# Edge stage of a graph attention kernel: a gather that waits for Q, and one weighed head moved from VectorE to GpSimd in every second pair

## The chip, the core and the metric

One core of a Trainium2 chip runs the whole program. Its engines work side by side, each through its own list of instructions, and wait for one another only by semaphores: TensorE (PE; loading of weights is shown as PEld), VectorE (DVE), ScalarE (ACT), GpSimd (POOL) and SyncE (SP), which issues DMAs. GpSimd and ScalarE issue DMAs too. The metric is the time of one execution on the device in microseconds (us), the median of several runs. Beside it stands one execution taken by the hardware profiler, whose trace is read here.

## What is computed

```python
N, D = x.shape                                   # 6250, 512
Q = (x @ Wq).reshape(N, H, d)                    # H = 8 heads of d = 64
K = (x @ Wk).reshape(N, H, d)
V = (x @ Wv).reshape(N, H, d)
src, dst = (edge_index[0], edge_index[1])        # 106250 edges, sorted by dst
score = jnp.einsum('ehd,ehd->eh', K[src], Q[dst]) * scale
score = jnp.exp(jnp.clip(score, -5.0, 5.0))[..., None]
msg = V[src] * score
wV = jax.ops.segment_sum(msg, dst, num_segments=N)
Z = jax.ops.segment_sum(score, dst, num_segments=N)
h_attn = (wV / (Z + 1e-06)).reshape(N, D)
h = x + h_attn                                   # then batch norm over the nodes, plus x,
                                                 # then layer norm of each row
```

All inputs are float32. Half of the edges go each way, and every node has a loop to itself.

## The kernel before

Three stages follow one another. `project` computes Q, K and V of all 49 tiles of 128 nodes and stores K and V side by side in `kv_d`, 4 KB a node. `attend` is the edge stage. `normalise` divides by Z and computes both norms. The change is in `attend`.

The edges lie in blocks of 128, one edge to a partition. A block that touches two tiles of destinations is visited twice, so there are 879 visits, taken in 440 pairs. A pair q uses slot q % 8 of a ring of eight in SBUF: `kv` holds for each of its two blocks the gathered K (512 numbers), V (512) and 8 weights. A name such as `s_g`, `s_seg`, `s_v` or `s_exp` is a family of eight semaphores, one for each slot; `s_qx` is a single one that counts pairs. The loop bodies are unrolled over the eight slots. For pair q the engines do this:

- GpSimd, `step` (line 752): two gathers, `gather(q, s, fills, 0)` and the same with u = 1, each an indirect DMA of 128 rows of 4 KB (line 747). Before the first it waits until the slot is free, which is when PE has accumulated pair q-8 (`s_seg`). Every fourth pair it copies indices. After the second gather it weighs, for even pairs only, one head of the pair that is five back (POOL_LAG): V times weight, `weigh`, line 710.
- PE, `step` (line 898): in step q it spreads the rows of Q over the edges of pair q+1 (two blocks, four matmuls into `q_ps`, line 915), once pair q has been multiplied, since `q_ps` has one buffer; this is counted in `s_qx`. Every second step it expands the bits of destinations (`mm_ps`, lines 925 and 927). Then it accumulates pair q-2 (`acc`, line 940), once all its heads are weighed: it waits for `s_v` to reach 3 a filling for even pairs (ScalarE, VectorE, GpSimd), 2 for odd ones. A record of the trace is half of such a float32 matmul, so one pair has eight.
- VectorE, `step` (line 783): it multiplies K by Q for pair q (line 791, waits for `s_g` and `s_qx`), clips the scores of q-1 (line 795), weighs heads of q-2 (line 710: three heads for even pairs, four for odd ones) and sums K times Q for pair q by head (line 802).
- ScalarE: exp of the scores (line 856), and four heads of both blocks weighed (line 842, eight instructions a pair); every second pair the matrices of zeros and ones (line 852), and for each tile that is complete the copy out of `acc`.

SyncE loads the tiles of Q, two of which are held. All of this order is written out by hand; nothing reorders it.

Of the kernel before, what the change touches and what calls it, by code (L numbers as in the profile page):

```python
# [32 lines left out]
N_NODES, DIM, HEADS = 6250, 512, 8  # L33
# [47 lines left out]
def wait_apart(eng, sem, value):  # L81


    if not isinstance(value, int):
        value = eng.snap(eng.to_reg(value))
        eng.wait_ge(sem, 1)
    wait(eng, sem, value)
# [538 lines left out]
def attend(nc, block, kv_d, q_d, lb_d, nb_d, xb_d, tabs, agg, rz, kv, first, x_first, s_first, s_slots, soft):  # L626
    lb, nb, q_tile, zeros, less, eps = first
    src_t, bits_row, cnt_row, ident = tabs
    with ExitStack() as ctx:
# [28 lines left out]
        s_nb, s_q = soft["s_nb"], soft["s_q"]  # L658
        s_qx, s_evc, s_evict = (soft[n] for n in ("s_qx", "s_evc", "s_evict"))
        s_rz = soft["s_rz_early"]  # L660
        POOL_LAG = 5
        LOOKAHEAD, LAG = 4, 3

        def pipeline(eng, step, head):
# [70 lines left out]
        def _(pool):  # L735
# [6 lines left out]
            def gather(q, s, fills, u):  # L742
                if u == 0:
                    if s % IDX_PAIRS == 0:
                        wait_apart(pool, s_idx[s // IDX_PAIRS], fills)
                    wait_apart(pool, s_seg[s], fills - 1)
                pool.indirect_dma_start(kv[:, s, u, 0:2 * DIM], None, kv_d,  # L747
                                        bass.IndirectOffsetOnAxis(idx[:, s, u:u + 1], 0),
                                        bounds_check=N_NODES - 1, oob_is_err=False
                                        ).then_inc(s_g[s], 16)  # L750

            def step(q, s, fills):
                p = q - POOL_LAG
                sp, fp = at(s, fills, -POOL_LAG)
                if there(q):
                    gather(q, s, fills, 0)
                if there(q + 2) and s % IDX_PAIRS == IDX_PAIRS - 2:
                    index(q + 2, *at(s, fills, 2))
                if there(q):
                    gather(q, s, fills, 1)  # L760
                if s % 2 and there(p):
                    wait_apart(pool, s_exp[sp], fp)
                    weigh(pool, sp, HEADS - POOL_HEADS, POOL_HEADS).then_inc(s_v[sp], 1)
            pool.wait_ge(soft["s_trc"], 1)
# [13 lines left out]
        def _(dve):  # L778
# [4 lines left out]
            def step(q, s, fills):  # L783
# [12 lines left out]
                                      ALU.min).then_inc(s_clip[s1], 1)  # L796
                if there(q - 2):
                    dve.wait_ge(s_exp[s2], f2)
                    weigh(dve, s2, ACT_HEADS, HEADS - ACT_HEADS - (POOL_HEADS if s % 2 == 0 else 0)).then_inc(s_v[s2], 1)
                if there(q):  # L800
                    dve.wait_ge(s_mul[s], fills)
                    dve.tensor_reduce(raw[:, s, :, :], heads(kv[:, s, :, 0:DIM]), AX.X,  # L802
# [78 lines left out]
        def _(pe):  # L881
# [16 lines left out]
            def step(q, s, fills):  # L898
# [32 lines left out]
                if there(c):  # L931
                    tiles = [pe.snap(tile_regs[(2 * sc + u) % PLACES], min_val=0, max_val=TILES - 1)
                             for u in range(2)]
                    pe.wait_ge(s_v[sc], (2 if sc % 2 else 3) * fc)
                    pe.wait_ge(s_evict, tiles[1] + 1)
                    for u in range(2):
                        par = tiles[u] % 2
# [442 lines left out]
```

## Time and profile before

| | us |
|---|---|
| median of 3 runs | 2098.77 |
| lowest, highest | 2097.2, 2105.61 |
| the profiled execution, time on the device | 2113.25 |
| the profiled execution, its span | 2111.5 |
| first to last start of VectorE's line 791 (edge stage) | 463.9 to 1959.1 |

| engine | busy us | share of the span |
|---|---|---|
| PE | 1918.3 | 91% |
| VectorE | 1696.9 | 80% |
| ScalarE | 1377.7 | 65% |
| GpSimd | 1249.1 | 59% |

The span is from the first to the last instruction of the profiled execution, 1.75 us less than its time on the device. The page sums up this execution in parts: busy time by engine, the chain of work that ended last, and groups of instructions by source line. The views of the trace give single instructions in order of time, the waits, and the busy time in any stretch. In a row, "[0.79 <-PE q_ps L915]" says that the engine had been idle for 0.79 us and that an instruction of line 915 on PE ended the wait, as far as the trace tells. The ends of matmuls are modelled. Where the profile names no releaser it writes "issue" or "remote".

### The profile page before, as it was taken

The page shows a single profiled execution, that of the slowest core. Times are in us where ns is not written, and L with a number is a line of the kernel's source. Part 1 is how long each engine was busy: PE and PEld are TensorE (multiplying, and loading weights), DVE is VectorE, ACT ScalarE, POOL GpSimd, SP SyncE. Part 2 cuts the span into 40 slices and gives each one's busy share as a digit, 9 for nine tenths or more (in the row PEclk, how much of TensorE's full clock was granted, in tenths as well). Part 3 has the DMA queues.
Part 4 walks back from the last instruction along what each step waited for, and adds up shares of the span by engine and source line. Part 5 has one row for each costly group of instructions (what it writes and reads, how often), then busy time and mean ns, then how long its engine had stood idle before and what let it go on. Part 6 is the DMA issues. An engine that isn't in the chain of part 4 may idle for free.

```text
span 2111.5 us, 41623 instructions
## 1 busy us (share of the span) xinstructions
PE 1918.3 (91%) x7904; PEld 1351.1 (64%) x8014; DVE 1696.9 (80%) x2454; ACT 1377.7 (65%) x4602; POOL 1249.1 (59%) x1473
## 2 busy tenths in 40 slices
PE   7999999989998998998899899898899899899887
PEld 4555555547776776776677677676676677677433
DVE  6676655538888888888888888888888888888988
ACT  0001000018887887887888888788788788788866
POOL 0106663026666666666666666666666666666657
PEclk9999999999999999999999999999999999999999
DMA  4648886358998898888888989898899899889607
GB/s 172 176 147 299 293 301 237 143 206 300 315 326 291 304 322 307 313 305 309 306 307 305 325 315 311 301 314 300 296 321 309 294 317 320 307 300 331 225 0 289
DMA packets 184521, 589.09 MB, mean 279 GB/s; under 512 B 28480, under 2 KB 30240, under 8 KB 184480
## 3 DMA queue, kind: packets, MB, share of 16 engines
q0 software_dynamic: 135904, 465.14, 63.5%
q1 hardware_dynamic: 45120, 121.69, 16.2%
q10 hardware_dynamic: 3456, 1.78, 0.3%
q8 instruction: 18, 0.29, 0.1%
q14 instruction: 23, 0.19, 0.0%
HBM read 535.27 MB, written 78.91 MB: 291 GB/s over the span
## 4 chain that ended last, share of the span: by engine, by line
PE 70%; DVE 16%; issue 7%; another core or an unknown queue 2%; ACT 2%; DMA 1%; POOL 1%; SPq 0%; DVEq 0%; ACTq 0%; POOLq 0%
PE q_ps L915 26%; PE places L342 20%; PE acc L940 19%; DVE kv L791 11%; PE mm_ps L925 2%; DVE stats L1278 1%; DVE agg L1262 1%; ACT agg L1189 1%; DVE raw L802 1%; PE mm_ps L927 1%; DVE agg L1271 1%; PE places L402 1%; PE banks L1132 1%; DMA kv<-kv_d,idx 1%
## 5 line engine op out<-in xcount | busy, mean ns | idle before, releaser
L747 POOL DMA_INDIRECT kv<-kv_d,idx x880 | 891.9, 1014 | 548.9 <-issue 214.0
L842 ACT ACTIVATE kv<-kv 128x64 f32<-128x64 f32 x3520 | 888.9, 335 | 14.3
L940 PE MATMUL acc<-kv,mm_sb 128*128 128x260 f32 x3520 | 852.1, 385 | 11.9 <-issue 4.4
L940 PEld LDWEIGHTS acc<-kv,mm_sb 128*128 128x128 f32 x3520 | 672.8, 192 | 114.3 <-issue 10.7
L791 DVE TENSOR_TENSOR kv<-q_ps,kv 128x1024 f32<-128x1024 f32 x440 | 536.4, 1219 | 214.7 <-PE q_ps L915 161.1
L915 PE MATMUL q_ps<-q_tile,mm_sb 128*128 x1760 | 550.0, 434 | 146.0 <-DVE kv L791 114.7
L802 DVE TENSOR_REDUCE raw<-kv 128x16 f32<-128x1024 f32 x440 | 532.7, 1211 | 0.0
L915 PEld LDWEIGHTS q_ps<-q_tile,mm_sb 128*128 128x128 f32 x1760 | 316.9, 190 | 285.3 <-DVE kv L791 193.6
L852 ACT ACTIVATE mm_sb<-mm_ps,less 128x1024 fp32r<-128x1024 f32 x220 | 241.5, 1098 | 66.2 <-remote 60.1
L710 DVE TENSOR_TENSOR kv<-kv 128x384 f32<-128x384 f32 (+1 forms) x440 | 271.8, 618 | 0.0
L856 ACT ACTIVATE kv<-raw 128x16 f32<-128x16 f32 x440 | 92.0, 209 | 197.9 <-DVE raw L795 181.8
L342 PE MATMUL places<-t_sb,s_sb 128*128 128x512 f32 (+1 forms) x552 | 185.5, 486 | 0.0
L435 ACT COPY p<-places 128x768 f32<-128x768 f32 x23 | 18.4, 799 | 247.8 <-PE places L342 247.8
L342 PEld LDWEIGHTS places<-t_sb,s_sb 128*128 128x128 f32 x552 | 104.8, 190 | 73.6 <-issue 66.5
L710 POOL TENSOR_TENSOR kv<-kv 128x128 f32<-128x128 f32 x220 | 91.7, 417 | 60.6 <-ACT kv L856 48.5
L342 PE MATMUL places<-w_sb,x_sb 128*128 128x512 f32 (+1 forms) x368 | 126.2, 486 | 0.0
L795 DVE TENSOR_SCALAR raw<-raw 128x16 f32<-128x16 f32 x440 | 103.6, 235 | 0.0
L342 PEld LDWEIGHTS places<-w_sb,x_sb 128*128 128x128 f32 x368 | 69.8, 190 | 49.1 <-issue 44.5
L925 PEld LDWEIGHTS mm_ps<-nb,lb 128*128 128x128 bf16 x880 | 50.5, 99 | 63.2 <-issue 63.2
L925 PE MATMUL mm_ps<-nb,lb 128*128 128x128 bf16 x880 | 88.6, 224 | 1.5 <-issue 1.5
L590 DVE TENSOR_TENSOR u<-places,p 128x768 f32<-128x768 f32 x23 | 22.0, 957 | 78.3 <-PE places L342 78.3
L440 ACT COPY kv_a<-places 128x256 f32<-128x256 f32 x23 | 8.6, 372 | 98.0 <-PE places L342 55.8
(171 smaller groups left out, 1354.1 us busy)
## 6 DMA issues: line engine op xcount, KB each, us to landing
q_tile<-q_d SPq DMA_DIRECT2D x49, 512.0 KB
kv<-kv_d,idx POOLq DMA_INDIRECT x880
kv_d<-kv_a SPq DMA_DIRECT2D x25, 512.0 KB
xb<-in_x POOLq DMA_DIRECT2D x49, 256.0 KB, 4.2
xb_d<-xb POOLq DMA_DIRECT2D x49, 256.0 KB, 3.7
out_rows<-agg SPq DMA_DIRECT2D x49, 256.0 KB, 2.1
x_sb<-in_xT SPq DMA_DIRECT2D x24, 512.0 KB, 8.1
q_d<-q_a SPq DMA_DIRECT2D x24, 512.0 KB
```

The source lines that it names most:

```text
L342: last = pe.matmul(out[:, cols], left[:, c, :], right[:, c, cols], start=fresh and c == 0, stop=c == DEEP - 1, skip_group_check=True)
L710: return eng.tensor_tensor(v, v, w, ALU.mult)
L747: pool.indirect_dma_start(kv[:, s, u, 0:2 * DIM], None, kv_d, bass.IndirectOffsetOnAxis(idx[:, s, u:u + 1], 0), bounds_check=N_NODES - 1, ...
L791: dve.tensor_tensor(k, q_ps[:, :, :], k, ALU.mult).then_inc(s_mul[s], 1)
L795: dve.tensor_scalar(raw[:, s1, :, :], raw[:, s1, :, :], -5.0, 5.0, ALU.max, ALU.min).then_inc(s_clip[s1], 1)
L802: dve.tensor_reduce(raw[:, s, :, :], heads(kv[:, s, :, 0:DIM]), AX.X, ALU.add).then_inc(s_red[s], 1)
L842: return act.activation(v, v, ACT.Copy, scale=kv[:, s, u, 2 * DIM + h:2 * DIM + h + 1])
L852: act.activation(mm_sb[:, sa // 2, :, :], mm_ps[:, :, :], ACT.Relu, bias=less[:, 0:1]).then_inc(s_mm[sa // 2], 1)
L856: act.activation(kv[:, s, :, 2 * DIM:KVW], raw[:, s, :, :], ACT.Exp).then_inc(s_exp[s], 1)
L915: last = pe.matmul(q_ps[:, u, :], one_hot(sb_, u, 1), part_q, start=(n == 0), stop=(n == 1))
L925: pe.matmul(mm_ps[:, 0, n * P:(n + 1) * P], lb[:, sa + n // 2, n % 2 * P:(n % 2 + 1) * P], nb[:, :], start=True, stop=True)
L940: last = pe.matmul(acc[:, bass.ds(par, 1), DIM - (1 - n) * HALF:DIM + n * HALF], m, kv[:, sc, u, DIM + n * HALF:DIM + (n + 1) * HALF], sta ...
```

## The change

Three things are altered in `attend`.

1. GpSimd's first gather of pair q waits, besides for its slot, until `s_qx` has reached q - 2, that is until PE has finished Q of pair q-3 (Q_LAG = 3).
2. GpSimd weighs its one head for every pair, where it did so for even ones only.
3. VectorE weighs three heads of every pair, where it weighed four of the odd ones, and PE's accumulation waits for three engines in every pair.

```diff
-        POOL_LAG = 5
+        POOL_LAG, Q_LAG = 5, 3
...
                     wait_apart(pool, s_seg[s], fills - 1)
+                    wait_apart(pool, s_qx, q + 1 - Q_LAG)
                 pool.indirect_dma_start(kv[:, s, u, 0:2 * DIM], None, kv_d,
...
-                if s % 2 and there(p):
+                if there(p):
                     wait_apart(pool, s_exp[sp], fp)
                     weigh(pool, sp, HEADS - POOL_HEADS, POOL_HEADS).then_inc(s_v[sp], 1)
...
-                    weigh(dve, s2, ACT_HEADS, HEADS - ACT_HEADS - (POOL_HEADS if s % 2 == 0 else 0)).then_inc(s_v[s2], 1)
+                    weigh(dve, s2, ACT_HEADS, HEADS - ACT_HEADS - POOL_HEADS).then_inc(s_v[s2], 1)
...
-                    pe.wait_ge(s_v[sc], (2 if sc % 2 else 3) * fc)
+                    pe.wait_ge(s_v[sc], 3 * fc)
```

GpSimd's list at the start of the loop over the eight slots, before. "DMA kv<-kv_d,idx" is a gather, "TENSOR_TENSOR kv<-kv 128x2x64" is one head of both blocks weighed, and the number behind `s_seg` or `s_exp` is the slot:

```order
L747 DMA kv<-kv_d,idx 128x1024 [waits s_idx0,s_seg0]
L747 DMA kv<-kv_d,idx 128x1024
L747 DMA kv<-kv_d,idx 128x1024 [waits s_seg1]
L747 DMA kv<-kv_d,idx 128x1024
L710 TENSOR_TENSOR kv<-kv 128x2x64 [waits s_exp4]
L747 DMA kv<-kv_d,idx 128x1024 [waits s_seg2]
```

The same place with the change; "L85 ISA" is a wait that stands by itself:

```order
L85 ISA [waits s_idx0,s_seg0]
L748 DMA kv<-kv_d,idx 128x1024 [waits s_qx]
L748 DMA kv<-kv_d,idx 128x1024
L710 TENSOR_TENSOR kv<-kv 128x2x64 [waits s_exp3]
L85 ISA [waits s_seg1]
L748 DMA kv<-kv_d,idx 128x1024 [waits s_qx]
L748 DMA kv<-kv_d,idx 128x1024
L710 TENSOR_TENSOR kv<-kv 128x2x64 [waits s_exp4]
```

A weighing now stands behind every two gathers, and every first gather waits for `s_qx` too.

VectorE's list in the same loop, from the multiplication into slot 2 on, before:

```order
L791 TENSOR_TENSOR kv<-q_ps,kv 128x2x512 [waits s_qx,s_g2]
L795 TENSOR_SCALAR raw<-raw 128x16 [waits s_red1]
L710 TENSOR_TENSOR kv<-kv 128x2x192 [waits s_exp0]
L802 TENSOR_REDUCE raw<-kv 128x16 [waits s_mul2]
L781 ISA
L791 TENSOR_TENSOR kv<-q_ps,kv 128x2x512 [waits s_qx,s_g3]
L795 TENSOR_SCALAR raw<-raw 128x16 [waits s_red2]
L710 TENSOR_TENSOR kv<-kv 128x2x256 [waits s_exp1]
L802 TENSOR_REDUCE raw<-kv 128x16 [waits s_mul3]
```

With the change:

```order
L792 TENSOR_TENSOR kv<-q_ps,kv 128x2x512 [waits s_qx,s_g2]
L796 TENSOR_SCALAR raw<-raw 128x16 [waits s_red1]
L710 TENSOR_TENSOR kv<-kv 128x2x192 [waits s_exp0]
L803 TENSOR_REDUCE raw<-kv 128x16 [waits s_mul2]
L782 ISA
L792 TENSOR_TENSOR kv<-q_ps,kv 128x2x512 [waits s_qx,s_g3]
L796 TENSOR_SCALAR raw<-raw 128x16 [waits s_red2]
L710 TENSOR_TENSOR kv<-kv 128x2x192 [waits s_exp1]
L803 TENSOR_REDUCE raw<-kv 128x16 [waits s_mul3]
```

Nothing moved; the weighing for an odd slot has three heads (192 columns a block) where it had four (256).

## Rows read from the trace of the kernel before

**Rows 1.** Page, part 4: the chain that ended last, shares of the span by line.

```profile
PE q_ps L915 26%; PE places L342 20%; PE acc L940 19%; DVE kv L791 11%; PE mm_ps L925 2%; DVE stats L1278 1%; DVE agg L1262 1%; ACT agg L1189 1%; DVE raw L802 1%; PE mm_ps L927 1%; DVE agg L1271 1%; PE places L402 1%; PE banks L1132 1%; DMA kv<-kv_d,idx 1%
```

**Rows 2.** VectorE's multiplications (line 791): count, ns min/median/max, first and last start.

```profile
L791 DVE TENSOR_TENSOR kv<-q_ps,kv x440: 1205/1223/1226, 463.9 to 1959.1; 128x1024 f32<-128x1024 f32 x147
```

**Rows 3.** Page, part 5: groups; busy us, mean ns of one | idle before, releaser.

```profile
L747 POOL DMA_INDIRECT kv<-kv_d,idx x880 | 891.9, 1014 | 548.9 <-issue 214.0
...
L710 POOL TENSOR_TENSOR kv<-kv 128x128 f32<-128x128 f32 x220 | 91.7, 417 | 60.6 <-ACT kv L856 48.5
```

**Rows 4.** Order of time, 1198 to 1216: start, us, engine, what [idle before <-releaser].

```profile
1201.30 1.22 DVE L791 TENSOR_TENSOR kv<-q_ps,kv 128x1024 f32<-128x1024 f32 x1 [0.82 <-PE q_ps L915]
1201.94 1.03 POOL L747 DMA_INDIRECT kv<-kv_d,idx  x1 [1.24 <-remote]
...
1202.58 1.20 PE L915 MATMUL q_ps<-q_tile,mm_sb 128*128 x4 [0.57 <-DVE kv L791]
...
1203.27 0.99 POOL L747 DMA_INDIRECT kv<-kv_d,idx  x1 [0.30 <-issue]
...
1204.07 1.92 PE L940 MATMUL acc<-kv,mm_sb 128*128 128x260 f32 x8
1204.11 1.22 DVE L791 TENSOR_TENSOR kv<-q_ps,kv 128x1024 f32<-128x1024 f32 x1
...
1205.63 1.28 PE L915 MATMUL q_ps<-q_tile,mm_sb 128*128 x4
...
1205.87 1.00 POOL L747 DMA_INDIRECT kv<-kv_d,idx  x1 [0.30 <-issue]
...
1206.89 0.41 POOL L710 TENSOR_TENSOR kv<-kv 128x128 f32<-128x128 f32 x1
1207.92 1.23 DVE L791 TENSOR_TENSOR kv<-q_ps,kv 128x1024 f32<-128x1024 f32 x1 [0.79 <-PE q_ps L915]
1208.55 1.03 POOL L747 DMA_INDIRECT kv<-kv_d,idx  x1 [1.24 <-remote]
```

**Rows 5.** Order of time, 644 to 652: two multiplications without a wait.

```profile
644.48 1.22 DVE L791 TENSOR_TENSOR kv<-q_ps,kv 128x1024 f32<-128x1024 f32 x1
...
647.41 1.22 DVE L791 TENSOR_TENSOR kv<-q_ps,kv 128x1024 f32<-128x1024 f32 x1
```

**Rows 6.** Order of time, 1158 to 1180: PE waits for GpSimd, then VectorE waits.

```profile
1161.32 0.42 POOL L710 TENSOR_TENSOR kv<-kv 128x128 f32<-128x128 f32 x1
...
1161.90 1.03 POOL L747 DMA_INDIRECT kv<-kv_d,idx  x1 [0.16 <-issue]
...
1162.04 2.02 PE L940 MATMUL acc<-kv,mm_sb 128*128 128x260 f32 x8 [0.58 <-POOL kv L710]
...
1163.70 1.29 PE L915 MATMUL q_ps<-q_tile,mm_sb 128*128 x4
...
1167.93 1.23 DVE L791 TENSOR_TENSOR kv<-q_ps,kv 128x1024 f32<-128x1024 f32 x1 [3.10 <-remote]
```

**Rows 7.** Order of time, 644 to 652: both engines weigh.

```profile
648.66 0.55 DVE L710 TENSOR_TENSOR kv<-kv 128x384 f32<-128x384 f32 x1
...
648.97 0.49 POOL L710 TENSOR_TENSOR kv<-kv 128x128 f32<-128x128 f32 x1
```

**Rows 8.** Order of time, 1036.5 to 1041.5: a gather that waited for acc.

```profile
1036.51 2.85 PE L940 MATMUL acc<-kv,mm_sb 128*128 128x260 f32 x8
...
1040.20 1.03 POOL L747 DMA_INDIRECT kv<-kv_d,idx  x1 [1.05 <-PE acc L940]
```

**Rows 9.** Order of time, 452 to 475: a gather of the ramp, and who waited.

```profile
459.86 1.02 POOL L747 DMA_INDIRECT kv<-kv_d,idx  x1 [0.16 <-POOL idx L739]
...
470.90 1.23 DVE L791 TENSOR_TENSOR kv<-q_ps,kv 128x1024 f32<-128x1024 f32 x1 [1.42 <-DMA kv<-kv_d,idx]
```

**Rows 10.** Stretches of the span: busy us by engine, PE clock, DMA share, GB/s.

```profile
core 0: us, PE busy (x) PEld busy (x) DVE busy (x) ACT busy (x) POOL busy (x), PEclk, DMA share, GB/s
...
1100.00:1300.00 200.00, 179.72 (x849) 139.67 (x863) 173.98 (x240) 165.80 (x577) 136.21 (x164) 1.00 0.90 315
```

## The prediction

> **What bounds the kernel now.** I read the chain that ended last first. Outside the projection (places) it runs through PE's q_ps (26%) and acc (19%) and VectorE's line L791 (11%) [rows 1]. So the edge stage, 440 pairs of gathers, is where both edits act. Its length is VectorE's first multiplication to its last, 463.9 to 1959.1: 1495.2 us, 3.406 us a pair [rows 2]. GpSimd has 880 gathers of 1.01 and 220 weighings of 0.42 in it, 2.24 us a pair, so it is the least busy of those that this change touches [rows 3].
>
> So I went to the order of time, where two pairs repeat every 6.62 us: multiplications at 1201.30, 1204.11 and 1207.92 [rows 4]. I call the pair multiplied at 1201.30 m. The step from m to m+1 is 2.81 and VectorE never waits: that is its own work with three heads. The same step with four heads is 2.93 where nothing waits (644.48 to 647.41) [rows 5]. The step from m+1 to m+2 is 3.81, and VectorE waits 0.79 in it. Two things are to be seen. First, Q of m+2 is given as complete at 1205.63 + 1.28 = 1206.91, and yet the multiplication that needs it begins at 1207.92. Second, PE stands still 0.57 before Q of m+1, so its own work is (6.62 - 0.57) / 2 = 3.03 us a pair. GpSimd meanwhile runs far ahead: the gather at 1208.55 is that of m+6, and it was held until its ring slot was free (pair m-2). Its head of pair m is weighed at 1206.89 to 1207.30, and PE reads it only when acc of m comes, two pairs after the acc of m-2 at 1204.07, so about 1210.7. That is 3.4 us of slack: GpSimd is off the path now.
>
> **VectorE, one head fewer in odd pairs.** 2.93 - 2.81 = 0.12 us in every second pair, 220 x 0.12 = 26 us of work. It lies in the step to m+2, where VectorE waits 0.79 afterwards, so it is worth nothing as long as that wait is longer: I take 0. At most it is 26 us.
>
> **GpSimd, one head more.** 220 more weighings of 0.42 = 92 us of GpSimd's time. A gather pair with its weighing costs 1.33 + 0.99 + 0.02 + 0.42 + 0.16 = 2.92 us (the 0.16 is the gap before a gather that needs no wait [rows 6]). That is under 3.406, so GpSimd does not become the bound by its work alone. Beside VectorE's weighing (648.66) GpSimd's took 0.49 instead of 0.42 [rows 7]: 0.07 us at most.
> The Trainium skill (SBUF — State Buffer, "SBUF: two separate sides") says that a VectorE instruction with two SBUF inputs and a GpSimd one that reads SBUF exclude each other for the whole instruction. By it a collision costs up to the 0.55 of VectorE's weighing, and one in every loop below would add 0.27 us a pair, 121 us in all; the row shows 0.07, and I go by the row.
>
> **The new wait on Q.** Behind it on GpSimd are queued both gathers of pair q and then the weighing of q-5, now of every pair. Today a first gather of q starts about when pair q-4 is multiplied (1207.92, then 1208.55 for m+6). With the edit it may not start before Q of q-3 is complete, about one pair later. The slack of 3.4 us is thereby spent, and a loop closes. PE's order is Q of k, then acc of k-3. So: Q of c+2 complete, then the gathers of c+5, then GpSimd's weighing of c, then acc of c, then Q of c+4. Two pairs, with these terms:
> - PE's end to the gather that waited for it: 1036.51 + 2.85 = 1039.36 to 1040.20, 0.84 [rows 8]
> - first gather to second 1.33 (1201.94 to 1203.27), second 0.99 [rows 4]
> - to the weighing 0.02, the weighing 0.42 (1206.87 to 1206.89 [rows 4], 0.42 [rows 6])
> - weighing's end to acc: 1161.74 to 1162.04, 0.30, the one place where PE waits for it [rows 6]
> - acc to the next Q 1.66 (1162.04 to 1163.70), that Q 1.29 [rows 6]
>
> The sum is 6.85 us for two pairs, 3.425 a pair. The path of today in undisturbed stretches is 6.62, so the new loop is the longer one and PE waits in it. Against the mean of 3.406 it gives 439 x 0.019 = +8 us. The mean is above 3.31 because of stretches like the one at 1167.93, where VectorE waits 3.10 [rows 6]; shorter runs of gathers may well remove them, and the comparison with the mean already grants that.
>
> **The open term: PE's late reports.** The 1.01 us between Q's end and the multiplication (1206.91 to 1207.92) stands, in every stretch that I read, where three or four gathers follow each other with gaps of 0.30; at 1163.70 + 1.29 = 1164.99 to 1167.93 it is 2.9, after a long run of gathers broken by one weighing alone. After one or two gathers (1203.78 to 1204.11) nobody waits. Now Q's report starts the gathers too, so every us of lateness enters the loop. The edit cuts the runs to two gathers, with breaks that I work out as 0.7 to 1.5 us. Lateness is bounded by 0 and by 0.9 for each loop. I take 0.1: near the rows after one or two gathers, and not 0, since the weighing at 1161.32, with the next gather 0.16 behind it, did not clear it. So 6.95 / 2 = 3.475, and 439 x 0.069 = **+30 us**. The profiled execution took 2113.25, so 2143.6 by its own scale; it stands 14.5 above the median of 2098.77, which makes **2129**.
>
> **Rivals.**
> *No change.* The loop closes but nothing is late, and acc to Q is the 1.56 of an unhindered one (1204.07 to 1205.63): 6.75 to 6.85, 3.375 to 3.425 a pair, -14 to +8 us: 2085 to 2107, mostly within 0.5%.
> *Faster.* The long runs of gathers are what costs today, through late reports. If they go and the weighing reaches PE in time, PE's 3.03 is the bound: 439 x 0.376 = -165, 1934. For it speaks the 0.79 of VectorE and the 0.57 of PE, against it the loop, each term of which is a row. It decides from a loop of 6.06 down; 0.79 would have to be missing from mine. Something between (3.36, about 2079) needs a loop only 0.13 shorter.
> *Much slower.* Reports stay late in both loops, by 0.5: 7.35 / 2 = 3.675, +118, 2217; at 0.9 it is +206. For it: the report before 1167.93 is late although a weighing stands in that run.
> *Data too late.* The second gather of q is now issued 3.16 after Q of q-3, and the multiplication of q stands 3 x 3.43 + 0.1 = 10.4 after it, which leaves 7.2 us. In the ramp a gather issued by 460.88 was waited for at 470.90, 10.0 us [rows 9], but there twelve gathers had been issued in 16 us with nothing to hold them; in the stage the DMA engines are busy 0.90 of the time, at 315 GB/s [rows 10]. From 7.2 on it decides; at 8.2 the three pairs take 11.4, 3.8 each, +173.
> The Trainium skill (DMA: Bandwidth & Descriptors, "Anatomy of one DMA — SWDGE (gpsimd) path") fits one DMA as 2.0 us and its bytes over 436 GB/s. By it a 512 KB gather lands in an estimated 3.2 us and this rival falls; no row here shows one alone, so I leave it its chance.
>
> **How the numbers follow.** My forecast (loop of 6.85 to 7.15, +10 to +74) has 0.42; no change 0.25; much slower 0.17; data too late 0.05; faster 0.11 (0.05 of it down to PE's bound). About 0.5%, 10.5 us, is what a measurement can tell from no change. So faster 0.11, same 0.25, slower 0.64. The range leaves out the faster cases and the upper half of the slow ones: 2086 to 2212.
>
> **What would show it.** Right, if PE waits before acc for GpSimd's weighing (now the one place in [rows 6]; then over a hundred, 0.2 to 0.5 us each), the first gather starts 0.84 after a Q's end, no run has more than two gathers without a weighing between, and VectorE's weighings are all of 384 columns with its idle time grown. Wrong, if acc never waits for GpSimd: then the term 0.30 or the order of PE is misread. If the multiplications still start 1 us after Q's end, the 0.1 is too small. If they wait for the DMA instead, it is the fourth rival.

## The result and the profile after

The changed kernel took 2179.16 us (median of 4 runs, 2178.64 to 2179.64) against 2097.98 us of the kernel before (2095.6 to 2105.61): 1.038 times as long, 95% interval 1.0354 to 1.0407, +81 us. The forecast was 2129 us. The direction was right, and the time lies inside the range of 2086 to 2212, but the loss is more than twice the +30 us that were worked out.

The page of the kernel after, part 4 and part 5: shares of the span in the chain that ended last, by engine and by line, then groups of instructions (busy us, mean ns of one | idle before, releaser). Line numbers are one higher than before from the new wait on.

```profile
PE 51%; issue 21%; POOL 18%; DVE 4%; POOLq 3%; DMA 3%; ACT 0%; SPq 0%; ACTq 0%
PE acc L941 20%; PE places L342 18%; POOL kv L748 12%; PE q_ps L916 10%; POOL kv L710 4%; POOLq L85 2%; DVE stats L1279 1%; DVE agg L1263 1%; POOL idx L739 1%; DMA kv<-kv_d,idx 1%; DVE agg L1272 1%; POOLq L748 1%; POOLq L78 1%; POOL agg L1102 1%; PE places L402 1%
```

```profile
L748 POOL DMA_INDIRECT kv<-kv_d,idx x880 | 893.3, 1015 | 562.4 <-PE q_ps L916 241.3
L941 PE MATMUL acc<-kv,mm_sb 128*128 128x260 f32 x3520 | 873.3, 391 | 188.0 <-POOL kv L710 181.0
...
L710 DVE TENSOR_TENSOR kv<-kv 128x384 f32<-128x384 f32 x440 | 243.5, 553 | 0.2 <-ACT kv L857 0.2
L710 POOL TENSOR_TENSOR kv<-kv 128x128 f32<-128x128 f32 x440 | 180.9, 411 | 20.1 <-ACT kv L857 9.2
```

The rows to compare are [rows 1] and [rows 3]. GpSimd was not in the chain's lines before. Now it has 18% of the chain, and another 21% is "issue", time in which the engine waited for nothing that the profile shows; it was 7% before. Two waits hold the loop of the prediction: GpSimd stood 241.3 us for Q before its gathers, and TensorE 181.0 us for GpSimd's weighing before acc. The weighings are the 440 of 128 and of 384 columns that the edit asks for, of 411 and 553 ns.

VectorE's multiplications, as in [rows 2] (count, ns min/median/max, first and last start):

```profile
L792 DVE TENSOR_TENSOR kv<-q_ps,kv x440: 1208/1225/1226, 466.3 to 2024.6; 128x1024 f32<-128x1024 f32 x147
```

466.3 to 2024.6 is 1558.3 us, 3.550 a pair, 63.1 us more than before. So the edge stage holds 63 of the 81 us. The start is 2.4 us later. The rest is that before's profiled execution (2113.25 us) stood 15.3 us above the median of 2097.98, where after's profiled execution (2178.88 us, span 2177.1) stands on its median.

What these multiplications waited for, in us and times:

```profile
  PE q_ps L916: 248.3, 303
...
  DMA kv<-kv_d,idx: 7.2, 11
```

They waited for Q and hardly for data, so the rival "data too late" is not what happened.

The order of time, 1169 to 1186 us, with the rows of the loop alone:

```profile
1171.11 1.22 DVE L792 TENSOR_TENSOR kv<-q_ps,kv 128x1024 f32<-128x1024 f32 x1 [0.80 <-PE q_ps L916]
...
1174.98 2.02 PE L941 MATMUL acc<-kv,mm_sb 128*128 128x260 f32 x8 [0.82 <-POOL kv L710]
...
1177.22 1.19 PE L916 MATMUL q_ps<-q_tile,mm_sb 128*128 x4 [0.22 <-issue]
...
1178.52 1.23 DVE L792 TENSOR_TENSOR kv<-q_ps,kv 128x1024 f32<-128x1024 f32 x1 [1.35 <-PE q_ps L916]
...
1179.25 1.02 POOL L748 DMA_INDIRECT kv<-kv_d,idx  x1 [1.41 <-PE q_ps L916]
...
1181.60 0.40 POOL L710 TENSOR_TENSOR kv<-kv 128x128 f32<-128x128 f32 x1
...
1182.30 2.02 PE L941 MATMUL acc<-kv,mm_sb 128*128 128x260 f32 x8 [0.77 <-POOL kv L710]
...
1183.96 1.27 PE L916 MATMUL q_ps<-q_tile,mm_sb 128*128 x4
...
1185.33 1.23 DVE L792 TENSOR_TENSOR kv<-q_ps,kv 128x1024 f32<-128x1024 f32 x1 [0.79 <-PE q_ps L916]
```

The loop, step by step: Q of 1177.22 ends at 1178.41 and the gather starts at 1179.25, 0.84 later. The second gather and the weighing follow, which ends at 1182.00. Acc starts at 1182.30, 0.30 behind it, after TensorE stood 0.77. Q follows at 1183.96, 1.66 behind acc. The multiplication that this Q releases is at 1185.33, two pairs and 6.81 us after the one at 1178.52. All of these are the terms of the prediction (0.84, 0.30, 1.66; 6.85 in all).

What it had not priced is in the same rows: from 1171.11 to 1178.52 it is 7.41. The acc of 1174.98 was followed by its Q only at 1177.22, 2.24 later and not 1.66, with 0.22 of "issue". This is where TensorE's program loop over eight pairs loads the mask of the next eight (`fetch`, a load of a register) and jumps back. In all of the 52 such places between the stage's ends acc to Q takes 2.23 us or more (median 2.25), and 1.66 is the median at the other odd pairs.

The second interruption comes once in 100 gathers:

```profile
1008.70 1.23 DVE L792 TENSOR_TENSOR kv<-q_ps,kv 128x1024 f32<-128x1024 f32 x1 [1.40 <-PE q_ps L916]
...
1012.40 1.00 POOL L748 DMA_INDIRECT kv<-kv_d,idx  x1 [1.94 <-issue]
...
1014.20 2.02 PE L941 MATMUL acc<-kv,mm_sb 128*128 128x260 f32 x8 [2.48 <-POOL kv L710]
...
1017.25 1.23 DVE L792 TENSOR_TENSOR kv<-q_ps,kv 128x1024 f32<-128x1024 f32 x1 [2.47 <-PE q_ps L916]
```

```profile
1189.34 1.01 POOL L748 DMA_INDIRECT kv<-kv_d,idx  x1 [2.04 <-issue]
...
1191.07 3.67 PE L941 MATMUL acc<-kv,mm_sb 128*128 128x260 f32 x8 [2.71 <-POOL kv L710]
...
1195.76 1.22 DVE L792 TENSOR_TENSOR kv<-q_ps,kv 128x1024 f32<-128x1024 f32 x1 [4.13 <-PE q_ps L916]
```

A gather starts after 1.94 or 2.04 us in which GpSimd waited for nothing that the profile shows. The gather at 835.19 has the same 2.04. From 835.19 to 1012.40 to 1189.34 it is 177 us, 50 pairs. The kernel before stalls in the same way, eight times in the stage; one of them:

```profile
1157.31 1.21 POOL L747 DMA_INDIRECT kv<-kv_d,idx  x1 [2.04 <-issue]
```

So the change did not bring the stalls, and they were not free before. There the two-pair step into which a stall falls, when no gather is issued, takes only 5.75 to 5.98 us; but the next takes 7.7 to 9.2, against a median of 6.68. In the changed kernel two pairs take 8.55 us at the stall of 1012.40 (1008.70 to 1017.25), 1.7 more than the loop. The one at 1189.34 cost 3.6: behind it the granted clock of TensorE was at the lower of its levels (1.2 GHz), and acc took 3.67 us instead of 2.02. Stretches of the span, with the columns of [rows 10]:

```profile
1191.00:1193.00 2.00, 1.93 (x5) 1.54 (x6) 0.63 (x1) 1.07 (x5) 1.70 (x2) 0.51 0.89 256
...
1195.00:1197.00 2.00, 2.00 (x13) 1.56 (x12) 1.24 (x3) 0.86 (x1) 0.50 (x1) 1.00 0.79 311
```

### The profile page after: what moved, and what is told of

It reads as the page before. It is cut to its first block, busy times and chain, and to the rows that moved or that the text cites. A ratio compares the mean times of both kernels' runs of the same rounds, so it can differ in the third digit from the quotient of the medians.

```text
span 2177.1 us, 43249 instructions
## 1 busy us (share of the span) xinstructions
PE 1934.9 (89%) x8013; PEld 1343.5 (62%) x8014; DVE 1688.3 (78%) x2454; ACT 1396.7 (64%) x4602; POOL 1339.0 (62%) x1693
## 3 DMA queue, kind: packets, MB, share of 16 engines
q10 hardware_dynamic: 3456, 1.78, 0.3%
## 4 chain that ended last, share of the span: by engine, by line
PE 51%; issue 21%; POOL 18%; DVE 4%; POOLq 3%; DMA 3%; ACT 0%; SPq 0%; ACTq 0%
PE acc L941 20%; PE places L342 18%; POOL kv L748 12%; PE q_ps L916 10%; POOL kv L710 4%; POOLq L85 2%; DVE stats L1279 1%; DVE agg L1263 1%; POOL idx L739 1%; DMA kv<-kv_d,idx 1%; DVE agg L1272 1%; POOLq L748 1%; POOLq L78 1%; POOL agg L1102 1%; PE places L402 1%
## 5 line engine op out<-in xcount | busy, mean ns | idle before, releaser
L748 POOL DMA_INDIRECT kv<-kv_d,idx x880 | 893.3, 1015 | 562.4 <-PE q_ps L916 241.3
L941 PE MATMUL acc<-kv,mm_sb 128*128 128x260 f32 x3520 | 873.3, 391 | 188.0 <-POOL kv L710 181.0
L941 PEld LDWEIGHTS acc<-kv,mm_sb 128*128 128x128 f32 x3520 | 645.4, 191 | 373.5 <-issue 284.6
L916 PE MATMUL q_ps<-q_tile,mm_sb 128*128 x1760 | 559.5, 439 | 17.4 <-issue 12.1
L916 PEld LDWEIGHTS q_ps<-q_tile,mm_sb 128*128 128x128 f32 x1760 | 330.4, 189 | 100.0 <-issue 34.0
L710 DVE TENSOR_TENSOR kv<-kv 128x384 f32<-128x384 f32 x440 | 243.5, 553 | 0.2 <-ACT kv L857 0.2
L710 POOL TENSOR_TENSOR kv<-kv 128x128 f32<-128x128 f32 x440 | 180.9, 411 | 20.1 <-ACT kv L857 9.2
L928 PE MATMUL mm_ps<-lb,nb 128*128 128x512 bf16 x220 | 83.6, 380 | 0.0
```

The costliest lines, as they stand in the source:

```text
L710: return eng.tensor_tensor(v, v, w, ALU.mult)
L916: last = pe.matmul(q_ps[:, u, :], one_hot(sb_, u, 1), part_q, start=(n == 0), stop=(n == 1))
L928: pe.matmul(mm_ps[:, 1, :], nb[:, :], lb[:, sa:sa + 2, :], start=True, stop=True).then_inc(s_t[sa // 2], 1)
L941: last = pe.matmul(acc[:, bass.ds(par, 1), DIM - (1 - n) * HALF:DIM + n * HALF], m, kv[:, sc, u, DIM + n * HALF:DIM + (n + 1) * HALF], sta ...
```

## The experiments

They ran in five groups, each on one chip and beside runs of the kernel before on it. The kernel before took 2114.6, 2113.2 and 2099.6 us in the first, third and fifth group, but 1913.1 and 1910.0 us in the second and fourth. I call these slower and faster groups. The expectations speak of kinds of chip, but the record gives the chip of the fourth group and of the fifth the same number, 6, and the kernel before took 1910.0 us in one and 2099.6 in the other; so the chip alone does not explain the two levels, and what does is not shown. The changed kernel itself ran in slower surroundings alone. The stage is VectorE's first multiplication to its last in the profiled execution.

| run | group | median us | before us | ratio, 95% | stage us |
|---|---|---|---|---|---|
| changed kernel, first | - | 2179.2 | 2098.0 | 1.038, 1.0354 to 1.0407 | 1558.3 |
| a1 Q wait alone | 1 | 2120.3 | 2114.6 | 1.0035, 1.0018 to 1.0051 | 1502.5 |
| a2 head alone | 1 | 2128.1 | 2114.6 | 1.0063, 1.004 to 1.0085 | 1499.1 |
| a3 Q of four back | 1 | 2120.5 | 2114.6 | 1.003, 1.0011 to 1.005 | 1505.0 |
| a5 Q wait, no head | 1 | 2108.8 | 2114.6 | 0.9967, 0.9951 to 0.9984 | 1488.1 |
| a7 jump moved | 2 | 2156.2 | 1913.1 | 1.1276, 1.1253 to 1.13 | 1534.0 |
| a8 head of odd pairs | 2 | 2175.2 | 1913.1 | 1.1369, 1.1345 to 1.1392 | 1555.9 |
| a9 a1, jump moved | 2 | 2119.1 | 1913.1 | 1.108, 1.1058 to 1.1102 | 1497.9 |
| a4 weighs four back | 2 | 2014.5 | 1913.1 | 1.0528, 1.0497 to 1.0558 | 1393.5 |
| b1 before | 3 | 2115.6 | 2113.2 | 1.001, 0.9998 to 1.0022 | 1488.9 |
| b2 changed kernel | 3 | 2176.4 | 2113.2 | 1.0299, 1.0281 to 1.0316 | 1555.0 |
| b3 head alone | 3 | 2122.1 | 2113.2 | 1.005, 1.0031 to 1.0068 | 1497.8 |
| b4 Q of four back | 3 | 2117.9 | 2113.2 | 1.0019, 1.0005 to 1.0033 | 1499.1 |
| c1 fetch early | 4 | 2146.3 | 1910.0 | 1.1237, 1.1216 to 1.1258 | 1525.9 |
| c3 fetch early, jump moved | 4 | 2148.6 | 1910.0 | 1.1245, 1.1223 to 1.1266 | 1526.4 |
| c2 two heads | 4 | 2225.9 | 1910.0 | 1.1654, 1.1631 to 1.1676 | 1606.1 |
| c4 head of odd pairs | 4 | 2176.8 | 1910.0 | 1.1394, 1.1365 to 1.1422 | 1556.3 |
| d1 before | 5 | 2099.0 | 2099.6 | 1.0005, 0.9976 to 1.0035 | 1475.8 |
| d2 head alone | 5 | 2092.8 | 2099.6 | 0.9966, 0.9943 to 0.999 | 1470.4 |

A thing to be seen first: kernels with the loop take nearly the same time in both kinds of group, as far as the runs go. No such kernel ran unchanged in both kinds. But a1 (slower group) and a9 (faster group) differ only in the place of TensorE's jump and took 2120 and 2119 us, and the changed kernel (slower groups) and a8 and c4 (faster groups) took 2176 and 2179, 2175 and 2177. The kernel before differs by 187 to 205 us. So kernels with the loop are compared below by their own times, across groups, and only the others by ratio.

### Each half alone

a1, the Q wait without the new weighing (against the changed kernel):

```
-                if there(p):
+                if s % 2 and there(p):
...
-                    weigh(dve, s2, ACT_HEADS, HEADS - ACT_HEADS - POOL_HEADS)
+                    weigh(dve, s2, ACT_HEADS, HEADS - ACT_HEADS - (POOL_HEADS if s % 2 == 0 else 0))
...
-                    pe.wait_ge(s_v[sc], 3 * fc)
+                    pe.wait_ge(s_v[sc], (2 if sc % 2 else 3) * fc)
```

> The first gather of a pair waits for the Q of the pair three back, as in the changed kernel; the weighing is left as before (GpSimd takes a head of the odd pairs alone). Theory A (a loop of two pairs: Q, 0.84 us, two gathers, the weighing of GpSimd, the additions, Q) : the loop runs through the odd pairs, and GpSimd still weighs in these, so nearly all of the loss is there: 3.45 to 3.55 us for a pair, 2135 to 2180 us. Rival B (the added head is what costs, by GpSimd's own time): about the time of before, 2098 us. Rival C (the gathers are issued too late for their data): also slow, but then the multiply of a pair waits for its gather and not for Q.

The pairs are misnamed there: behind the gathers of an odd pair q GpSimd weighs pair q-5, which is even. So in a1, as in the kernel before, it weighs a head of the even pairs.

a2, b3 and d2, the weighing without the Q wait:

```
-                    wait_apart(pool, s_qx, q + 1 - Q_LAG)
```

> GpSimd weighs one head of every pair and VectorE three, and the gathers don't wait for a Q. Theory A: no loop through the gathers, so at most the time of before, and less if the weighing of every pair breaks up the long runs of gathers in which TensorE's reports came late: 2.95 to 3.4 us for a pair, 1900 to 2098 us. Rival B (the added head costs): 2135 to 2180 us. Rival C: the time of before.

> GpSimd's head of every pair alone, without the Q wait. If the chip is like the second (before about 1913 us): by GpSimd's own sum 2.92 us for a pair against 2.85 before, 0 to 2 % slower than before. If it is like the first: 1.006 again. Rival B (the added head costs by itself): 1.04 or more.

> GpSimd's head of every pair alone, no Q wait. On the faster kind of chip: GpSimd's own sum goes from 2.85 to 2.92 us for a pair, 0 to 2 % slower than before (1910 to 1950 us); over 4 % slower would mean that the added weighing costs more than its time. On the slower kind: 1.005 again.

Neither half costs anything like the whole: +0.35% and, over three groups, +0.6, +0.5 and -0.3%. Together they cost 3.0 to 3.8%. Both my theory A (nearly all in a1) and rival B (nearly all in a2) missed. Order of time in a1:

```profile
1251.34 0.99 POOL L748 DMA_INDIRECT kv<-kv_d,idx  x1 [1.60 <-PE q_ps L916]
...
1254.35 2.02 PE L941 MATMUL acc<-kv,mm_sb 128*128 128x260 f32 x8 [0.73 <-POOL kv L710]
...
1256.02 1.28 PE L916 MATMUL q_ps<-q_tile,mm_sb 128*128 x4
...
1257.42 1.22 DVE L792 TENSOR_TENSOR kv<-q_ps,kv 128x1024 f32<-128x1024 f32 x1 [0.92 <-PE q_ps L916]
...
1258.15 0.99 POOL L748 DMA_INDIRECT kv<-kv_d,idx  x1 [1.51 <-PE q_ps L916]
...
1265.03 0.99 POOL L748 DMA_INDIRECT kv<-kv_d,idx  x1 [1.67 <-PE q_ps L916]
```

The loop is there, gather to gather 6.81 (1251.34 to 1258.15) and 6.88, with its 0.84 behind Q and TensorE waiting 0.73 for the weighing. But that is all it costs: 1502.5 us of stage over 219.5 steps are 6.845 each, hardly more than the undisturbed step. Theory A had the loop right and its price (2135 to 2180) wrong: the interruptions are missing. With the weighing in the even pairs only, the loop runs through these; the question was why the interruptions spare it.

### Taking the loop apart

a3 and b4 change one number, a5 takes GpSimd's weighing out (VectorE does all four heads; the last five pairs stay as in the changed kernel), a4 weighs one pair earlier:

```
a3  -        POOL_LAG, Q_LAG = 5, 3
    +        POOL_LAG, Q_LAG = 5, 4
a4  -        POOL_LAG, Q_LAG = 5, 3
    +        POOL_LAG, Q_LAG = 4, 3
a5  -                if there(p):
    +                if isinstance(p, int) and PAIRS - POOL_LAG <= p < PAIRS:
```

> The changed kernel with one number changed: the gather waits for the Q of the pair four back. Theory A: the same steps now span three pairs, 6.85 / 3 = 2.3 us for a pair, so the loop is no bound; what is left is TensorE at 3.0 to 3.1 us for a pair if its reports stay prompt (1930 to 1990 us), or about the time of before if they come late again (2050 to 2100 us). Rival B (GpSimd's added head): the time of the changed kernel, 2179 us. Rival C (gathers too late): a pair more of room, also about the time of before.

> The changed kernel with the gather waiting for the Q of the pair four back. Like the second chip: the loop spans three pairs and is no bound, so within 2 % of the run with the head alone. Like the first: 1.003 again.

> The changed kernel, but VectorE weighs all four of its heads and GpSimd none (only in the last five pairs as in the changed kernel); the gather still waits for the Q of the pair three back. Theory A: nothing leads from the gathers to the additions but the data, so the loop is gone: 3.0 to 3.3 us for a pair, 1930 to 2060 us. Rival B (the added head): about the time of before, 2098 us. Rival C (the wait makes the gathers late for their data): still 2150 to 2180 us, with the multiply waiting for its gather.

> The changed kernel, but GpSimd weighs the pair four back and not five, the Q wait unchanged. Theory D: the loop then spans three pairs (6.85 / 3 = 2.3 us for a pair) and is no bound; what remains is what bounded the runs without this loop, 0.995 to 1.01 of before. It would be 0.92 to 0.95 if TensorE's reports stayed prompt. Rival B (the added weighing, one a pair, is what costs): 1.038.

a3, b4 and a5 give the loss back beside the kernel before. a4 takes 162 us less than the changed kernel, though in its faster group it is 5% slower than the kernel before. So the loss needs both the wait at three back and a weighing of GpSimd five back: the loop as it was written down. In a5 the gathers wait for the same Q as in the changed kernel and nothing is lost, which rules out rival C. a4's 0.995 to 1.01 was missed; b4 gave a3's result again. But the 3.0 to 3.3 us a pair of theory A came in none of the slower groups' runs. The reason is in a3's order of time:

```profile
1219.07 1.28 PE L916 MATMUL q_ps<-q_tile,mm_sb 128*128 x4
...
1219.81 1.00 POOL L748 DMA_INDIRECT kv<-kv_d,idx  x1 [0.30 <-issue]
...
1220.82 0.42 POOL L710 TENSOR_TENSOR kv<-kv 128x128 f32<-128x128 f32 x1
...
1221.50 1.22 DVE L792 TENSOR_TENSOR kv<-q_ps,kv 128x1024 f32<-128x1024 f32 x1 [1.06 <-PE q_ps L916]
...
1225.83 1.29 PE L916 MATMUL q_ps<-q_tile,mm_sb 128*128 x4
...
1228.38 1.22 DVE L792 TENSOR_TENSOR kv<-q_ps,kv 128x1024 f32<-128x1024 f32 x1 [1.18 <-PE q_ps L916]
```

Q of 1219.07 ends at 1220.35 and the multiplication begins at 1221.50, 1.15 later; the next time it is 1.26. These are the late reports of TensorE that stood in [rows 4], and a single weighing between the gathers does not clear them. In the changed kernel the multiplication starts 0.10 behind Q (1183.96 + 1.27 = 1185.23, then 1185.33). Summed over all multiplications that waited, what goes beyond 0.10 is 226 us in the kernel before, 241 in a3 and 231 in a5, but 7 in the changed kernel and 22 in a1. So in the slower groups a kernel without the loop (3.35 to 3.43 us a pair) has late reports, and one with the loop does not and is held by the loop. Why the reports are late, and that the breaks between short runs of gathers are what keeps them prompt, is argued from these rows and not shown.

a4 ran in a faster group. There its multiplications wait for data:

```profile
  DMA kv<-kv_d,idx: 98.8, 69
  PE q_ps L916: 19.3, 33
```

```profile
kv<-kv_d,idx POOLq DMA_INDIRECT x880, 5.8
```

98.8 of its waiting is for gathers, which landed 5.8 us after their issue (median), and 19.3 us for Q. With the Q wait at three back, and no loop to hold the pace down, the data come too late: the rival "data too late" is real, but only at 3.17 us a pair. The Trainium skill (DMA: Bandwidth & Descriptors, "Anatomy of one DMA — SWDGE (gpsimd) path") makes that an estimated 3.2 us by its fit for one DMA; here, with other traffic beside it, it was 5.8, and the measurement decides.

### Odd pairs or more work

a8, and c4 as its repetition: the Q wait with half of the weighing as in a1, but of the odd pairs.

```
-                if s % 2 and there(p):
+                if s % 2 == 0 and there(p):
...
-                    weigh(dve, s2, ACT_HEADS, HEADS - ACT_HEADS - (POOL_HEADS if s % 2 == 0 else 0))
+                    weigh(dve, s2, ACT_HEADS, HEADS - ACT_HEADS - (POOL_HEADS if s % 2 else 0))
...
-                    pe.wait_ge(s_v[sc], (2 if sc % 2 else 3) * fc)
+                    pe.wait_ge(s_v[sc], (3 if sc % 2 else 2) * fc)
```

> The Q wait as in the changed kernel, and as much weighing for GpSimd as before (a head of every other pair), but of the odd pairs and not of the even ones. Theory D: the loop now runs through the odd pairs with the jump of TensorE in it, so 25 to 30 us more than the run with the Q wait alone: 1.016 to 1.022 of the time of before (that run gave 1.0035). Rival B (the amount of weighing on GpSimd decides): 1.0035, as in that run, since the amount is the same.

> The Q wait with GpSimd's half of the weighing on the odd pairs, beside the kernel before on this chip. Theory D: 2170 to 2180 us, as on the other chip, 50 us more than with the even pairs and about the changed kernel's time. Rival B (the amount of weighing decides): 2120 us on this chip, the earlier difference being one of the chips.

2175 and 2177 us, with the same amount of work on every engine as a1's 2120. That is all of the changed kernel's loss, and 55 us more than with the even pairs. The comparison does not rest on two groups: a9, even pairs again, ran beside a8 and took 2119.1. (The ratios forecast were those of a slower group; the times are what to compare.) So the 92 us of added weighing on GpSimd cost nothing; what costs is that now the odd pairs have a weighing too, and the loop moves to them. The interruptions are there again:

```profile
1173.37 2.02 PE L941 MATMUL acc<-kv,mm_sb 128*128 128x260 f32 x8 [0.81 <-POOL kv L710]
...
1175.61 1.19 PE L916 MATMUL q_ps<-q_tile,mm_sb 128*128 x4 [0.22 <-issue]
...
1180.69 2.02 PE L941 MATMUL acc<-kv,mm_sb 128*128 128x260 f32 x8 [0.75 <-POOL kv L710]
...
1182.35 1.28 PE L916 MATMUL q_ps<-q_tile,mm_sb 128*128 x4
...
1187.75 1.01 POOL L748 DMA_INDIRECT kv<-kv_d,idx  x1 [2.08 <-issue]
...
1189.59 3.58 PE L941 MATMUL acc<-kv,mm_sb 128*128 128x260 f32 x8 [2.83 <-POOL kv L710]
```

Acc to Q takes 2.24 at the jump and 1.66 else, as in the changed kernel, and the stall of 2.08 before the gather at 1187.75 goes straight to acc, which waited 2.83. The stalls come at the gathers of even pairs, in front of the weighing of an odd one. In a1 no weighing follows these gathers, but the 1.5 to 1.7 us in which GpSimd waits for the next Q, and these take most of the stall up. Two gathers of its rows, one after the other:

```profile
1161.25 1.01 POOL L748 DMA_INDIRECT kv<-kv_d,idx  x1 [1.85 <-issue]
1162.56 0.99 POOL L748 DMA_INDIRECT kv<-kv_d,idx  x1 [0.30 <-issue]
```

The second is the first gather of the next pair, and it did not have to wait for its Q.

### The load of the mask and the jump

a7 moves TensorE's jump one step (the body now runs from the second step of eight to the first of the next), a9 does so in a1, c1 moves the load, c3 both:

```
a7, a9, c3
-            for q in range(-LOOKAHEAD, RING):
+            for q in range(-LOOKAHEAD, RING + shift):
...
-                for s in range(RING):
-                    step(i * RING + s, s, i + 1)
+                for s in range(shift, RING + shift):
+                    step(i * RING + s, s % RING, i + 1 + s // RING)
...
-            pipeline(pe, step, PE_HEAD)
+            pipeline(pe, step, PE_HEAD, shift=1)
c1, c3 (these two lines from the end of TensorE's step to ahead of its additions)
                 if s == RING - 1:
                     fetch(q // RING + 2 if isinstance(q, int) else fills + 1)
```

> The changed kernel with TensorE's loop of eight pairs begun one step later, so that its jump back stands ahead of the Q of an even pair and not of an odd one; the instructions are the same otherwise. Theory D (the loop through Q, gathers, weighing and additions is the bound and lies on the odd pairs, and the 0.55 us of the jump come on top of it once in eight pairs): the jump now stands where TensorE waits anyway, so 30 us less than the changed kernel: 1.022 to 1.028 of the time of before, against its 1.038. Rival B (it is the added work of GpSimd, with its weighing of every pair): 1.038, unchanged.

> The Q wait alone, with TensorE's jump moved one step later, ahead of the Q of an even pair, where the loop of this kernel runs. Theory D: the jump comes on top of the loop once in eight pairs, so 25 to 30 us more: 1.016 to 1.022 of before. If the place of the jump doesn't matter: 1.0035.

> The changed kernel, with TensorE's load of the next eight pairs' mask placed ahead of the additions of the eighth step instead of behind them; the jump back stays where it is. If the load and the jump in a row are the 0.59 us between the additions and the next Q: the load goes under the wait for GpSimd, some 0.3 to 0.45 us less once in eight pairs, 15 to 25 us less than the changed kernel (2152 to 2164 us). If the jump alone is the 0.59 us: no change, 2176 us.

> The same, and the jump one step later (ahead of the Q of an even pair). Theory D: nothing of either is left on the odd pairs' loop, 30 us less than the changed kernel, 2143 to 2150 us; the run with the jump moved alone gave 2156.

a7 gained 20 to 23 us against the changed kernel, less than the 30 expected. c1 gained 30 to 33, more than the 15 to 25 expected, and c3 no more than c1, inside its own range: nearly the whole of the interruption is gone when the load is under TensorE's wait. In c1's order of time acc to Q at the jump is 1.79 (1157.11 to 1158.90) and 1.66 else:

```profile
1157.11 2.02 PE L943 MATMUL acc<-kv,mm_sb 128*128 128x260 f32 x8 [0.81 <-POOL kv L710]
...
1158.90 1.20 PE L916 MATMUL q_ps<-q_tile,mm_sb 128*128 x4
...
1163.99 2.02 PE L943 MATMUL acc<-kv,mm_sb 128*128 128x260 f32 x8 [0.77 <-POOL kv L710]
...
1165.65 1.26 PE L916 MATMUL q_ps<-q_tile,mm_sb 128*128 x4
```

Apart, the two are small, and together they are more than their sum. In a7 the load stands by itself in the loop and acc to Q takes 1.80 there (median of 52 places, against 1.66), so the load costs 0.14. The jump by itself costs 0.12 in c1 (median 1.78) and 0.16 in a9 (1.82). In a row they take 0.58 us. a9 was expected 25 to 30 us above a1 and came out 1.2 below: even the 9 us of the 0.16 are not to be seen in its time, and why is not shown. For c1, 0.58 - 0.13 = 0.45 us 53 times, the turns of TensorE's program loop, is 24 of the 30 to 33 us. Another 7 lie in GpSimd's stalls: behind none of them did the clock fall in c1 (every addition took under 0.49 us), where it fell behind four in the changed kernel (26 additions of over 0.6 us, the longest 0.80). What decided that is not shown: the waits before acc were as long in c1, up to 2.73 us. The lines of acc in c1, then in the changed kernel (duration ns min/median/max):

```profile
L943 PE MATMUL acc<-kv,mm_sb x3520: 381/382/483, 472.8 to 1996.6; 128*128 128x260 f32 x196
```

```profile
L941 PE MATMUL acc<-kv,mm_sb x3520: 380/382/797, 477.4 to 2032.3; 128*128 128x260 f32 x196
```

That a1 is spared by load and jump is explained too: in it they stand before the Q of an odd pair, where TensorE then waits for the weighing of an even one.

### The slope of the loop

c2, with two heads of every pair weighed by GpSimd and two by VectorE:

```
-POOL_HEADS = 1
+POOL_HEADS = 2
```

> The changed kernel with two heads of every pair weighed by GpSimd and two by VectorE. Theory D: GpSimd's weighing is in the loop, once in two pairs, so each 0.1 us of it costs 22 us; at 0.42 us for one head and an estimated 0.65 to 0.8 for two, 50 to 85 us more than the changed kernel, 2226 to 2261 us. If GpSimd counted by its sum (2.92 us for a pair, 3.15 to 3.3 with two heads, still under the 3.5 us of a pair): no change, 2176 us.

```profile
L941 PE MATMUL acc<-kv,mm_sb 128*128 128x260 f32 x3520 | 874.6, 392 | 239.4 <-POOL kv L710 232.0
...
L710 POOL TENSOR_TENSOR kv<-kv 128x256 f32<-128x256 f32 x440 | 274.8, 625 | 19.8 <-ACT kv L857 9.0
```

GpSimd's weighing went from 411 to 625 ns, 0.214 us once in two pairs: 220 x 0.214 = 47 us. Measured: 2225.9, 47 to 50 us more than the changed kernel. It costs one for one, while GpSimd is busy 64% of the span. The forecast counted with 0.65 to 0.8 us for two heads; 0.625 lies just below, and so does 2225.9 below the 2226.

### The two levels of the kernel before

b1, b2 and d1 are the kernels before and after once more.

> The kernel before, for a trace on the chip of this group of runs. Theory E (TensorE's reports come late in long runs of gathers on some chips and not on others, and where they don't the kernel is bound by GpSimd at 2.9 us for a pair): about 2100 us with the multiply waiting 0.8 us behind Q in every other pair, or about 1913 us with no such wait. Rival F (the fast chip is faster in the data, its gathers land sooner): 1913 us with reports as late as in the first trace.

> The changed kernel. Theory D (it is bound by the loop through Q, gathers, weighing and additions, in which no report is late): 2175 to 2185 us on every chip, so 1.038 of before on a chip like the first and 1.135 to 1.145 on one like the second. Rival F: on a chip like the second it gains as before does, 1990 us.

> The kernel before. On a chip of the faster kind (1910 us) theory E expects two pairs in about 5.75 us, the multiply within 0.2 us of the end of Q also in long runs of gathers, and GpSimd the busiest; rival F expects Q reported as late as in the first trace and gathers that land sooner. On a chip of the slower kind: 2100 to 2116 us as before.

All three fell into slower groups. The changed kernel repeats at 2176.4. So there is no trace of the kernel before in a faster group, and the cause of its two levels stays open. What speaks for the late reports as the difference: the kernels with the loop, which have hardly any, differ little between the groups; a4, without the loop, has its multiplications wait 19.3 us for Q in all, where b1 and a3 wait 159 and 198 us; and before's 1910 to 1913 us lie near the 1934 that the rival "faster" worked out for reports in time. That is an argument and not shown.

## Why the prediction was right and wrong

**Right.** The chain of steps, its order and each size: 0.84, 1.33 and 0.99, 0.02, 0.42, 0.30, 1.66 and 1.29 are all found again, and two undisturbed pairs take 6.8 to 6.9 us (mean 6.87) where 6.85 stood. That VectorE's head is worth nothing, and that GpSimd's added 92 us cost nothing as a sum: a8 and c4 show it, which leave the even pairs' head with VectorE and take the changed kernel's time. TensorE's 181 us before acc, the 0.84 after Q, runs of two gathers and 384 columns were to be seen, and are.
The rule of the Trainium skill (SBUF — State Buffer, "SBUF: two separate sides") would have added up to 121 us, and the prediction put 0.07 for a collision against it. The trace agrees with the rule; what did not come are the collisions. Of the changed kernel's 440 weighings by GpSimd only 12 lie beside one of VectorE's, and the other 428 take 402 to 425 ns. One that began 0.04 us behind VectorE's, whose own ended at 2028.90:

```profile
2028.38 0.78 POOL L710 TENSOR_TENSOR kv<-kv 128x128 f32<-128x128 f32 x1 [1.75 <-ACT kv L857]
```

It ended 0.26 us after VectorE's, and the one of 0.49 us in [rows 7], which began later into VectorE's, 0.25. So "0.07 at most" misread that row: a collision costs up to 0.37 us. That there were few was luck as far as the prediction goes, which never asked where the two weighings fall in the loop.

**Wrong, the open term.** Late reports were given 0.1 a loop, 22 us. It is 0 in the undisturbed loop, where the multiplication starts 0.10 and the gather 0.84 behind Q.

**Wrong, the comparison of an undisturbed loop with a disturbed mean.** The step "against the mean of 3.406 it gives +8 us, and the comparison with the mean already grants that" is the one that failed. The 6.85 is a step with nothing in the way; 3.406 was a mean over all stretches, GpSimd's stalls with what follows them included: the wait of 3.10 at 1167.93 [rows 6] stands 10 us behind the stall of 1157.31. Like with like, the 6.62 of an undisturbed stretch against the 6.85, would have been 439 x 0.115 = +50 us, and both numbers stood in the prediction. The prediction put every interruption of the new loop at nothing, taking it that they would go with the long runs of gathers. The late reports went, and two kinds stayed that this loop cannot absorb:
- load and jump of TensorE, once in eight pairs, 0.55 us each: 27 us outside the stalls. Before, TensorE stood 0.57 in every two pairs [rows 4] and the 0.58 went there: acc to Q takes 2.51 us at these places and 2.48 to 2.50 at the other odd pairs (medians). c1 shows this part by experiment.
- GpSimd's stall once in 100 gathers, 8 times, 1.6 to 3.6 us each, four of them with the clock down: 21 us. Before, the stalls had their cost inside the 3.406; in the new loop the prediction counted none. This part is read from the traces (it is there in a8 and absent in a1); no run takes the stalls away.

These sums are over the starts of all 440 multiplications, against 6.86 us for two pairs. So the working was 8 + 22 = 30. The trace has 8 for the loop at 6.85 and 2 for its 6.86, 0 for the reports, 27 and 21, and 4 spread over single stretches that I have not assigned: 62 of the 63.

**Wrong, the transfer to the median.** The prediction took off 14.5 us because before's profiled execution stood that far above its median. A kernel held by a loop of fixed steps showed less spread (2178.64 to 2179.64, against 2095.6 to 2105.61), and its profiled execution is its median. This is 15 of the 50 us between 2129 and 2179; 33 are the 63 of the stage against 30, and 2 its later start.

**The rivals.** "No change" gave the right loop (6.75 to 6.85) with the same fault. "Much slower" (2217) lies nearer to the measured time than the forecast, with a wrong cause: the reports were prompt. "Faster" is refuted for this lag, and in the slower groups for every variant tried, but for the 0.3% of a5 and, in one group of three, of the head alone. "Data too late" was seen only at a pace of 3.17 us a pair (a4); here it is 7.2 us of waiting in all.

## What to carry to other kernels

When an edit closes a loop, its undisturbed period is the floor and not the forecast: add every periodic interruption of an engine in the loop (a program loop's register load and jump, a queue's stall), as often as it comes, or compare undisturbed stretches with undisturbed ones. Which half of the work the loop runs through can matter more than how much work is added: with the Q wait, the same weighing took 2120 us in the even pairs and 2175 in the odd ones. Of the versions tried none beats the kernel before by more than 0.3%, and each with the Q wait at three back that ran in a faster group lost 5% or more there.

## What the runs showed of the hardware

- The kernel before takes 1910 to 1913 us in two groups and 2098 to 2116 us in three and in the first runs, and the chip of one group of each kind has the same number. Kernels bound by the loop that differ little from each other differ by under 0.2%. A ratio of two kernels can thus hang on where they ran: the Q wait is 1.0035 in one group (a1) and, with the jump moved, 1.108 in another (a9).
- A load of a register followed by the jump of TensorE's program loop takes 0.58 us (acc to Q 2.24 and not 1.66); the load alone 0.14 (a7), the jump alone 0.12 (c1) to 0.16 (a9).
- GpSimd stands 1.6 to 2.1 us before every 100th gather in the kernel before, in the changed kernel and in every other run with the Q wait but a4; in a4 and with the head alone (a2, b3, d2) some of these gaps are shorter.
- GpSimd's weighing of one head takes 0.40 to 0.42 us by itself. Where it began inside VectorE's weighing and got longer, it ended 0.25 to 0.26 us after that one's end, so it took up to 0.78 us in the changed kernel and 0.85 in a4.
- TensorE's granted clock fell to 0.51, the lower of its two levels, for some 3 us after TensorE had stood for 2.71 us, and did not after 2.48 us (acc of 2.02 us at 1014.20). The length of the wait alone does not decide: in the changed kernel it also fell after 2.58, 2.69 and 2.74 us and not after 2.72, and in c1 it fell after none of eight waits of 2.42 to 2.73 us.
